# Other hand-written orders for all five engines, and A's transfers ahead of the small vectors

## The chip, the core and the metric

One Trainium2 core runs the whole program. The metric is the device time of one execution in microseconds; lower is better. The program is one launch: a stretch for the first batch, a loop over six middle batches, a stretch for the last.

## The reference

Input x is (8, 1024, 256): eight batches of 1024 rows. All is computed in float32.

```
xn = layernorm(x)                                     # 1e-5
# attention branch, 16 heads of depth 16, no softmax
q = elu(xn @ Wq + bq) + 1 ; k = elu(xn @ Wk + bk) + 1 ; v = xn @ Wv + bv
k = k / sqrt(sum(k*k over a head) + 1e-6)
att = (q k^T) v per head ;  y = xn + (att @ Wo + bo)
a = (y - mean(y)) / sqrt(var(y) + 1e-6) * gamma + beta
# feed-forward branch, three blocks of two quantised linears with low-rank parts
lin_l(h) = h @ dequant(qweights[l], scales[l])^T + biases[l] + (h @ A[l]^T) @ B[l]^T
h = xn
for blk in 0..2:  h = h + lin_{2blk+1}( gelu( layernorm(lin_{2blk}(h)) ) )
out = x + a + h
```

A is `lora_a` (6, 32, 256), B is `lora_b` (6, 256, 32). The codes `qweights` are (6, 256, 256) integers.

## The kernel before

**Tiling.** A batch's 1024 rows lie as eight tiles of 128 rows (`X`, `XN`); a half `h` is four of them, 512 rows. The feed-forward branch works on transposed activations: two 128-channel parts (`m` or `k` = 0, 1) by 512 rows, one PSUM bank each (`FB[h][m]`). Each operand of its products is split into a rounded part and the rest (`xTh`/`xTl`, `hTh`/`hTl`, `gh`/`gl`, `WTh`/`WTl`); `first_high`/`second_high` are eight products of 512 columns with the rounded part, `first_low`/`second_low` four with the rest. Block `j` is `first_*`, squares, variance and its root, normalise, gelu, `second_*`, residual.

**A block's hand-overs.** TensorE `first_high`, `first_low`; ScalarE `square` (L620) for both parts; GpSimd `add_squares` (L417); TensorE `turn_squares` (L1570); VectorE `ffn_var` (L911, L914); GpSimd `ffn_root` (L392); TensorE `spread_rstd` (L1578); ScalarE `rb_copy` (L626); VectorE `ffn_normalise` (L923); ScalarE `gelu` (L630); rounding `g_higher` on VectorE for part 0 (L937) and on ScalarE for part 1 (L635); rest `g_lower` (L262) mostly on GpSimd, some on VectorE; TensorE `second_high` (L1478), `second_low` (L1484); VectorE `ffn_residual` (L932); `h_higher` (VectorE L941, ScalarE L639), `h_lower` (L267). The last block's second product is made row-wise: `rows_state` (L1538), `rows_high` (L1551), `rows_low` (L1561), and `finish` (L1043) adds it into `RES`.

**Attention.** TensorE `project_k(p)` (L1594) for pair p of tiles, ScalarE `k_exp` (L647), VectorE `k_elu` (L948), ScalarE `k_square` (L651), VectorE `k_sum`, `k_rstd` (eleven small instructions), `k_hat` (L982); TensorE `add_g(t)` (L1605) sums K^T xn in bank 4, ScalarE `g_copy` (L656); `make_vk`, `block_diagonal`, `make_m`, `m_copy` build one matrix M per batch; `project_q(h, m)` (L1616), `q_exp` (L663), `q_elu` (L989) make qT; `attend(p)` (L1649) is qT by M. VectorE `att_y(p)` (L1009 to L1020) adds `XNB` and takes the statistics, GpSimd `ln2_root`, VectorE `att_result` (L1029, L1035). GpSimd `base_xn(p)` (L412) makes `XNB` = xn + bo.

**Next batch.** `ln1_statistics`, `ln1_mean_var` (VectorE), `ln1_root` (GpSimd), `ln1_normalise` (ScalarE L611), `xt` (TensorE L1471), `xt_copy` (ScalarE L601, L602) and `xt_lower` (VectorE L1053) of batch i+1 run inside batch i.

**Start.** Weights come once. SyncE issues X, `lora_b`, scales, codes and the projection weights; ScalarE issues seven small vector transfers (`load_vectors`, which waits for one GpSimd constant) and then the four of A (`load_lora`, L580) into `Y`. GpSimd `dequantise` (L430, L435), TensorE `weight_transpose` (L1739 transposes the codes' tile, L1745 adds B A from `lbT` and `Y`), ScalarE `weights_high`, VectorE `weights_low`. `keep_busy` (L1657) is four filler products. `qk_sums` (L1719, L1720) is the column means of Wq and Wk.

**Order.** Nothing is scheduled by the hardware beyond each engine's own list: the functions `head`, `body`, `tail` of every engine name the calls one by one, and semaphores make them wait. Each engine runs its list in order, so a wait holds all behind it. Short-lived results share three rotating PSUM banks and a fourth, the side bank; `HEAD_USES`, `BODY_USES`, `TAIL_USES` list the uses in TensorE's order, `take` (a wait in TensorE for the reader of the bank's last use) and `rotating` derive bank and count from them.

## Time and profile before

| | before |
|---|---|
| median of 3 runs | 616.52 us (616.03 to 617.02) |
| the profiled execution's own time | 616.88 us |
| its span | 615.2 us, 10218 instructions |
| TensorE matmuls | 590.7 us, 96% |
| TensorE weight loads | 498.3 us, 81% |
| VectorE | 526.9 us, 86% |
| ScalarE | 402.8 us, 65% |
| GpSimd | 373.9 us, 61% |
| granted TensorE clock | full in all 40 slices |
| DMA | 29.0 MB, 47 GB/s over the span |

The span is the distance from the first to the last recorded instruction; what lies around it belongs to the execution's time too. A busy share of TensorE near 100% says that it is never without an instruction, not that each is as short as it can be: an instruction that waits inside the pipeline counts as busy. The chain that ended last passes TensorE for 70% of the span, ScalarE for 9%, GpSimd for 7% and VectorE for 6%. In a row of the timeline the columns are the start, the time from the first start to the last end of the merged instructions, the engine, the line, the operation and its tiles, the count, and in brackets the idle time before it with what ended it. In the waits the columns are the total, the number and the longest.

### The profile page before, as it was taken

The numbers are of one execution on the slowest core, as the hardware profiler recorded it, in microseconds if no ns is written. First come the engines' busy times: TensorE is split into PE (matmuls) and PEld (weight loads), VectorE is DVE, ScalarE is ACT, GpSimd is POOL, SyncE is SP. The second block draws the span as 40 slices with busy tenths as digits, with TensorE's granted clock in tenths as the row PEclk, the third lists the DMA queues.
The fourth block names the chain that finished last, engine by engine and source line by source line (L and its number), as shares of the span: only waits on it lengthen the run. The fifth ranks groups of instructions, "written<-read, shape, count | busy, mean of one in ns | idle before, by whom it ended". The sixth has DMA issues, their size and how long they took to land.

```text
span 615.2 us, 10218 instructions
## 1 busy us (share of the span) xinstructions
PE 590.7 (96%) x3285; PEld 498.3 (81%) x3285; DVE 526.9 (86%) x1164; ACT 402.8 (65%) x619; POOL 373.9 (61%) x361
## 2 busy tenths in 40 slices
PE   6999999999999999999999999999999999999986
PEld 5778879778897889868797788978889688987865
DVE  3679899798888989889897988979898898989797
ACT  2776656848667577766768576684876667775552
POOL 5745766557644766457665575556754576746574
PEclk9999999999999999999999999999999999999999
DMA  9103000500032000500004000230004000030001
GB/s 241 62 2 136 1 2 35 170 2 0 1 125 80 0 0 18 180 6 0 0 35 170 0 0 0 87 118 0 0 0 173 32 0 0 34 102 1 0 2 69
DMA packets 11461, 29.00 MB, mean 47 GB/s; under 512 B 2593, under 2 KB 4273, under 8 KB 11441
## 3 DMA queue, kind: packets, MB, share of 16 engines
q1 hardware_dynamic: 10960, 28.35, 13.7%
q10 hardware_dynamic: 480, 0.41, 0.3%
q8 instruction: 10, 0.16, 0.1%
q14 instruction: 11, 0.08, 0.0%
HBM read 20.37 MB, written 8.39 MB: 47 GB/s over the span
## 4 chain that ended last, share of the span: by engine, by line
PE 70%; ACT 9%; POOL 7%; DVE 6%; issue 6%; DMA 1%; ACTq 1%; DVEq 0%; POOLq 0%
PE bank L1478 19%; PE bank L1484 9%; PE bank L1594 7%; PE bank L1605 7%; PE bank L1649 6%; PE bank L1551 4%; PE bank L1616 4%; PE bank L1570 3%; ACT fw L630 3%; POOL gl L262 2%; ACT L630 2%; PE bank L1578 2%; PE bank L1561 2%; PE bank L1538 2%; PE bank L1471 2%
## 5 line engine op out<-in xcount | busy, mean ns | idle before, releaser
L262 POOL TENSOR_TENSOR gl<-fw,gh 128x512 fp32r<-128x512 f32 x80 | 104.2, 1319 | 49.4 <-DVE gh L937 37.5
L417 POOL TENSOR_TENSOR sqs<-fw 128x512 f32<-128x512 f32 x48 | 62.8, 1309 | 73.8 <-ACT fw L620 73.7
L620 ACT ACTIVATE fw<-bank,b1c 128x512 f32<-128x512 f32 x96 | 62.3, 686 | 57.8 <-PE bank L1484 57.8
L630 ACT ACTIVATE fw<-fw,vec 128x512 f32<-128x512 f32 x96 | 74.6, 808 | 14.2 <-DVE fw L923 13.9
L923 DVE SCALAR_TENSOR_TENSOR fw<-bank,b1c,rb 128x512 f32<-128x512 f32 x96 | 67.7, 745 | 16.1 <-ACT rb L626 15.8
L267 POOL TENSOR_TENSOR hTl<-hT,hTh 128x512 fp32r<-128x512 f32 x40 | 54.1, 1368 | 39.8 <-ACT hTh L639 33.0
L392 POOL TENSOR_TENSOR rsf<-vef,neghalf 128x4 f32<-128x4 f32 x48 | 50.6, 1055 | 43.7 <-DVE vef L914 43.0
L1605 PE MATMUL bank<-K,XN 128*128 128x256 f32 x256 | 61.7, 382 | 0.0
L1649 PE MATMUL bank<-M,qT 128*128 128x256 f32 x256 | 59.4, 379 | 0.0
L392 POOL TENSOR_TENSOR rs<-ve,neghalf 128x2 f32<-128x2 f32 (+1 forms) x48 | 41.9, 874 | 22.8 <-DVE ve L1020 17.1
L1605 PEld LDWEIGHTS bank<-K,XN 128*128 128x128 f32 x256 | 46.5, 190 | 7.6 <-DVE K L982 2.0
L1649 PEld LDWEIGHTS bank<-M,qT 128*128 128x128 f32 x256 | 47.2, 190 | 6.1
L626 ACT ACTIVATE rb<-bank 128x512 f32<-128x512 f32 x48 | 28.3, 592 | 35.1 <-PE bank L1578 34.2
L1478 PE MATMUL bank<-gh,WTl 128*128 128x512 f32 x128 | 42.5, 412 | 1.4 <-DVE gh L937 1.4
L1478 PE MATMUL bank<-hTh,WTl 128*128 128x512 f32 x128 | 43.1, 418 | 0.0
L601 ACT ACTIVATE xTh<-bank 128x512 fp32r<-128x512 f32 x32 | 19.2, 599 | 35.8 <-PE bank L1471 35.7
L911 DVE TENSOR_REDUCE bank<-bank 128x4 f32<-128x512 f32 x48 | 33.4, 697 | 10.3 <-PE bank L1570 9.4
L412 POOL TENSOR_TENSOR XNB<-XN,bo_r 128x512 f32<-128x512 f32 x32 | 41.7, 1303 | 0.0
L1478 PE MATMUL bank<-hTh,WTh 128*128 128x512 f32 x128 | 40.3, 396 | 0.0
L1478 PE MATMUL bank<-gh,WTh 128*128 128x512 f32 x128 | 40.2, 395 | 0.0
L1484 PE MATMUL bank<-gl,WTh 128*128 128x512 f32 x128 | 36.9, 410 | 0.0
L1578 PE MATMUL bank<-ident,rsf 128*128 128x128 f32 x192 | 29.0, 274 | 6.8 <-POOL rsf L392 6.8
(157 smaller groups left out, 1593.0 us busy)
## 6 DMA issues: line engine op xcount, KB each, us to landing
X<-in_L_attn_x_dram SPq DMA_DIRECT2D x16, 512.0 KB, 6.7
RES<-in_L_attn_x_dram SPq DMA_DIRECT2D x16, 512.0 KB, 4.3
out_dram<-RES SPq DMA_DIRECT2D x14, 512.0 KB, 2.7
XNB<-in_L_ffn_qweights_dram SPq DMA_DIRECT2D x2, 512.0 KB, 6.6
out_dram<-RES SPq DMA_DIRECT2D x4, 256.0 KB, 2.1
RES<-in_L_ffn_qweights_dram SPq DMA_DIRECT2D x1, 512.0 KB, 8.8
Y<-in_L_ffn_lora_a_dram ACTq DMA_DIRECT2D x4, 96.0 KB, 6.6
Wp<-in_L_attn_Wq_dram SPq DMA_DIRECT2D x1, 256.0 KB, 7.6
```

Of the source, the lines that this page charges most:

```text
L262: engine.tensor_tensor(gl[:, h, m, :], fw[:, h, m, :], gh[:, h, m, :].bitcast(F32), ALU.subtract).then_inc(g_low[h][m], 1)
L267: engine.tensor_tensor(hTl[m][:, half(h)], hT[m][:, half(h)], hTh[m][:, half(h)].bitcast(F32), ALU.subtract).then_inc(h_low[h][m], 1)
L392: return pool.tensor_tensor(dst, var, neghalf[:, 0:n], ALU.pow)
L417: pool.tensor_tensor(sqs[:, h, :], fw[:, h, 0, :], fw[:, h, 1, :], ALU.add).then_inc(sqs_ready[h], 1)
L620: act.activation(fw[:, h, m, :], FB[h][m][:], ACT.Square, bias=b1c[:, m, j:j + 1]).then_inc(sq_ready[h], 1)
L630: act.activation(fw[:, h, m, :], fw[:, h, m, :], ACT.Gelu, bias=lnb[:, m, j:j + 1], scale=lng[:, m, j:j + 1]).then_inc(g_ready[h], 1)
L923: dve.scalar_tensor_tensor(fw[:, h, m, :], FB[h][m][:], b1c[:, m, j:j + 1], rb[:, h, :], ALU.add, ALU.mult).then_inc(yn_ready[h], 1)
L1478: pe.matmul(FB[h][m][:], w[:, l, k, m * P:(m + 1) * P], high, start=(k == 0 and n == 0), stop=False)
L1484: ins = pe.matmul(FB[h][m][:], WTh[:, l, k, m * P:(m + 1) * P], low, start=False, stop=(k == NC - 1))
L1594: ins = pe.matmul(RB[r][:, t * D:(t + 1) * D], x_[k][:, (2 * p + t) * P:(2 * p + t + 1) * P], w[:, k, D:2 * D], start=(n == 0), stop=(n == ...
L1605: ins = pe.matmul(AB[:, c * D:(c + 1) * D], XN[:, t, c * P:(c + 1) * P], K[:, t, :], start=(t == 0 and c == 0), stop=(t == NT - 1), skip_g ...
L1649: ins = pe.matmul(RB[r][:, t * D:(t + 1) * D], qT[c][:, (2 * p + t) * P:(2 * p + t + 1) * P], M[:, c, :], start=(c == 0), stop=(c == NC - 1))
```

## The change

Every engine's three lists get another order; the calls in each list are the same ones, so no instruction and no transfer is added or removed. The three lists of bank uses follow TensorE's new order. In the first batch ScalarE issues `load_lora` ahead of `load_vectors`. SyncE's first-batch list has Wv, Wk and codes 1 ahead of Wq, and bo and gamma later. The middle batch:

```diff
 BODY_USES = [
-    ("k", 0), ("k", 1), ("var", 0, 0), ("rs", 0, 0), ("k", 2), ("k", 3),
+    ("k", 1), ("k", 0), ("var", 0, 0), ("rs", 0, 0), ("k", 2), ("k", 3),
...
@@ sync, head
                 load_small()
                 load_codes(0)
-                load_row(bo_r, bo.unsqueeze(0))
+                load_projection(2, Wv, w_v)
+                load_projection(1, Wk, w_k)
+                load_codes(1)
                 load_projection(0, Wq, w_q)
                 load_out()
-                load_projection(1, Wk, w_k)
-                load_codes(1)
+                load_x(0, 1)
+                load_row(bo_r, bo.unsqueeze(0))
+                load_codes(2)
                 load_row(gamma_r, gamma.unsqueeze(0))
-                load_x(0, 1)
-                load_projection(2, Wv, w_v)
-                load_codes(2)
@@ gpsimd, body
                 ffn_root(i, 0, 0)
+                base_xn(i, 0, BODY)
+                base_xn(i, 1, BODY)
                 add_squares(i, 1, 0)
-                base_xn(i, 0, BODY)
+                base_xn(i, 2, BODY)
                 ffn_root(i, 1, 0)
...
@@ scalar, head
+                load_lora()
                 load_vectors()
-                load_lora()
@@ scalar, body
                 gelu(i, 0, 1, 0)
-                g_copy(i)
                 gelu(i, 0, 1, 1)
                 g_higher(i, 0, 1, 1)
                 rb_copy(i, 1, 1, BODY)
+                g_copy(i)
                 gelu(i, 1, 1, 0)
                 gelu(i, 1, 1, 1)
                 g_higher(i, 1, 1, 1)
+                ln1_normalise(i + 1, 0, BODY)
                 h_higher(i, 0, 1, 0)
                 q_exp(i, 1, 1, BODY)
-                ln1_normalise(i + 1, 0, BODY)
                 m_copy(i, BODY)
@@ vector, body (as it stands after the change)
                 ffn_residual(i, 0, 1, 0, BODY)
                 ln1_mean_var(i + 1, 1)
                 ffn_residual(i, 0, 1, 1, BODY)
                 h_lower(dve, i, 0, 1, 0)
                 h_higher(i, 0, 1, 1)
                 ffn_residual(i, 1, 1, 0, BODY)
                 ffn_residual(i, 1, 1, 1, BODY)
                 h_higher(i, 1, 1, 1)
                 q_elu(i, 1, 1, BODY)
@@ tensor, head
-                keep_busy()
                 lb_transpose()
                 keep_busy()
                 keep_busy()
+                vec_transpose()
                 keep_busy()
-                vec_transpose()
+                keep_busy()
                 weight_transpose(0)
...
+                project_k(0, 3, HEAD)
                 weight_transpose(4)
-                project_k(0, 3, HEAD)
+                second_high(0, 0, 0, HEAD)
+                project_q(0, 1, 0, HEAD)
+                second_low(0, 0, 0)
+                weight_transpose(5)
                 project_q(0, 0, 1, HEAD)
-                weight_transpose(5)
@@ tensor, body
                 add_g(i, 0, BODY)
+                add_g(i, 1, BODY)
                 first_high(i, 0, 1, BODY)
...
-                add_g(i, 1, BODY)
                 turn_squares(i, 0, 1, BODY)
...
+                add_g(i, 5, BODY)
                 turn_squares(i, 1, 1, BODY)
                 spread_rstd(i, 0, 1, BODY)
-                add_g(i, 5, BODY)
                 add_g(i, 6, BODY)
+                project_q(i, 1, 1, BODY)
                 add_g(i, 7, BODY)
                 spread_rstd(i, 1, 1, BODY)
-                project_q(i, 1, 1, BODY)
```

In the last batch TensorE's list moves one q projection between `spread_rstd(i, 1, 0)` and `second_high(i, 0, 0)`; GpSimd's has base_xn(0) to (2) early, base_xn(3) ahead of the second block's g_lower, and `ffn_root(i, 0, 2)` ahead of `add_squares(i, 1, 2)`. In the first batch TensorE's `spread_rstd(0, 0, 0)` moves ahead of `project_k(0, 2)`, and VectorE's `ffn_normalise(0, 0, 2, *)` ahead of `xt_lower(1, 0, 1)`, its `g_higher(0, 0, 2, 0)` ahead of `att_y(0, 2)`.

## Rows read from the trace of the kernel before

**Rows 1.** Busy time of each engine by stretch; then granted clock, DMA share, GB/s

```profile
229.00:301.40 72.40, 71.12 (x397) 60.04 (x396) 63.81 (x142) 49.66 (x77) 44.44 (x41) 1.00 0.13 43
...
591.20:615.20 24.00, 16.75 (x109) 14.12 (x107) 20.14 (x48) 8.04 (x11) 12.72 (x12) 1.00 0.11 44
```

**Rows 2.** Waits of TensorE: total us, times, longest us

```profile
PE bank L1578 <- POOL rsf L392: 6.8, 9, 1.0
```

**Rows 3.** Timeline of the start, the two issuing queues and TensorE

```profile
3.69 1.83 ACTq L580 DMA_DIRECT2D Y<-in_L_ffn_lora_a_dram  x4
...
5.37 1.66 SPq L282 DMA_DIRECT2D Wp<-in_L_attn_Wk_dram  x1
...
6.66 3.62 PE L1657 MATMUL bank<-mean_w,ident 128*128 128x128 f32 x24
...
10.21 0.29 PE L1676 MATMUL bank<-ident,vec_rows 13*128 13x13 f32 x2
...
13.11 1.13 PE L1745 MATMUL bank<-lbT,Y 128*128 128x256 f32 x4 [1.62 <-DMA Y<-in_L_ffn_lora_a_dram]
...
14.95 1.88 PE L1719 MATMUL bank<-Wp,mean_w 128*128 128x512 f32 x4
```

**Rows 4.** DMA issues: KB each, us from issue to landing

```profile
Y<-in_L_ffn_lora_a_dram ACTq DMA_DIRECT2D x4, 96.0 KB, 6.6
...
Wp<-in_L_attn_Wk_dram SPq DMA_DIRECT2D x1, 256.0 KB, 8.2
```

**Rows 5.** Busy time by stretch at the start, columns as in rows 1

```profile
10.00:14.00 4.00, 2.02 (x13) 1.51 (x12) 2.17 (x7) 1.04 (x3) 2.36 (x3) 1.00 1.10 301
```

**Rows 6.** Timeline of TensorE in the first batch and one middle batch

```profile
38.06 0.70 PE L1616 MATMUL bank<-xTh,Wqkl 128*128 128x512 f32 x2 [0.54 <-issue]
...
44.66 0.66 PE L1739 MATMUL bank<-ident,RES 128*128 128x128 f32 x4 [0.84 <-DVE K L948]
...
90.51 0.66 PE L1538 MATMUL bank<-ident,hT 128*128 128x128 f32 x4 [0.75 <-DVE fw L923]
...
94.29 0.38 PE L1551 MATMUL bank<-WTl,gh 128*128 128x256 f32 x1 [0.52 <-DVE gh L937]
...
228.24 0.66 PE L1570 MATMUL bank<-ident,sqs 128*128 128x128 f32 x4 [0.31 <-POOL sqs L417]
...
262.22 0.62 PE L1578 MATMUL bank<-ident,rsf 128*128 128x128 f32 x4 [0.78 <-POOL rsf L392]
263.02 0.70 PE L1478 MATMUL bank<-gh,WTl 128*128 128x512 f32 x2 [0.18 <-DVE gh L937]
...
295.24 0.63 PE L1478 MATMUL bank<-hTh,WTl 128*128 128x512 f32 x2
295.70 0.63 PE L1478 MATMUL bank<-hTh,WTh 128*128 128x512 f32 x2
...
300.68 0.66 PE L1570 MATMUL bank<-ident,sqs 128*128 128x128 f32 x4 [0.31 <-POOL sqs L417]
```

**Rows 7.** Timeline of ScalarE, then VectorE, in the same middle batch

```profile
291.64 0.62 ACT L639 ACTIVATE hTh<-hT 128x512 fp32r<-128x512 f32 x1
...
294.16 2.07 ACT L611 ACTIVATE XN<-X,sh,rs 128x256 f32<-128x256 f32 x4
...
270.55 0.68 DVE L262 TENSOR_TENSOR gl<-fw,gh 128x512 fp32r<-128x512 f32 x1
...
286.88 1.82 DVE L262 TENSOR_TENSOR gl<-fw,gh 128x512 fp32r<-128x512 f32 x1
```

**Rows 8.** Timeline of the last batch: TensorE, GpSimd, VectorE

```profile
552.70 0.71 PE L1478 MATMUL bank<-gh,WTl 128*128 128x512 f32 x2 [0.34 <-DVE gh L937]
...
599.71 0.62 PE L1578 MATMUL bank<-ident,rsf 128*128 128x128 f32 x4 [0.98 <-POOL rsf L392]
...
597.31 1.28 POOL L412 TENSOR_TENSOR XNB<-XN,bo_r 128x512 f32<-128x512 f32 x1
...
611.31 1.27 DVE L1043 TENSOR_TENSOR RES<-bank,RES 128x512 f32<-128x512 f32 x2
```

More of the change, by code:

```diff
@@ L499, in body, with tail @@
                 ffn_root(i, 0, 0)
+                base_xn(i, 0, BODY)
+                base_xn(i, 1, BODY)
                 add_squares(i, 1, 0)
-                base_xn(i, 0, BODY)
+                base_xn(i, 2, BODY)
+                ffn_root(i, 1, 0)
+                g_lower(pool, i, 0, 0, 0)
+                g_lower(pool, i, 0, 0, 1)
+                g_lower(pool, i, 1, 0, 0)
+                h_lower(pool, i, 0, 0, 0)
+                h_lower(pool, i, 0, 0, 1)
+                h_lower(pool, i, 1, 0, 0)
+                h_lower(pool, i, 1, 0, 1)
+                add_squares(i, 0, 1)
+                add_squares(i, 1, 1)
+                ffn_root(i, 0, 1)
+                base_xn(i, 3, BODY)
+                ffn_root(i, 1, 1)
+                g_lower(pool, i, 0, 1, 1)
+                ln1_root(i + 1, 0)
+                g_lower(pool, i, 1, 1, 0)
+                g_lower(pool, i, 1, 1, 1)
+                h_lower(pool, i, 0, 1, 1)
+                add_squares(i, 0, 2)
+                ln2_root(i, 0)
+                ffn_root(i, 0, 2)
+                ln1_root(i + 1, 1)
+                add_squares(i, 1, 2)
+                ffn_root(i, 1, 2)
+                g_lower(pool, i, 0, 2, 1)
+                g_lower(pool, i, 0, 2, 0)
+                ln2_root(i, 1)
+                g_lower(pool, i, 1, 2, 1)
+                g_lower(pool, i, 1, 2, 0)
+                ln2_root(i, 2)
+                ln2_root(i, 3)
+            def tail(i):
+                add_squares(i, 0, 0)
+                base_xn(i, 0, TAIL)
+                ffn_root(i, 0, 0)
+                base_xn(i, 1, TAIL)
+                base_xn(i, 2, TAIL)
+                add_squares(i, 1, 0)
                 ffn_root(i, 1, 0)
@@ L1397, in tail @@
                 ffn_residual(i, 1, 1, 1, TAIL)
+                q_elu(i, 1, 1, TAIL)
                 att_y(i, 0, TAIL)
@@ L1819, in head @@
                 turn_squares(0, 0, 2, HEAD)
+                xt(1, 0, 0, HEAD)
+                first_high(0, 1, 2, HEAD)
+                spread_rstd(0, 0, 2, HEAD)
+                first_low(0, 1, 2)
                 xt(1, 0, 1, HEAD)
-                first_high(0, 1, 2, HEAD)
-                first_low(0, 1, 2)
-                spread_rstd(0, 0, 2, HEAD)
                 attend(0, 2, HEAD)
```

339 lines of the change are left out of this document (148 added, 191 removed), and 18 rows, old and new, of tables (BODY_USES, HEAD_USES, TAIL_USES).

## The prediction, made before the changed kernel ran

> **What bounds the kernel now.** I read the stretches first. In a middle batch TensorE is busy 71.12 of 72.40 us, VectorE 63.81, ScalarE 49.66, GpSimd 44.44, with the DMA engines at a share of 0.13 and the granted clock at 1.00 (the upper level, 2.4 GHz); in the last 24 us TensorE falls to 16.75 while VectorE is busy 20.14 [rows 1]. So three regions have different limits: the start (transfers), the stream up to the last batch (TensorE), the last 20 us (VectorE). TensorE's waits come next: the largest is for the reciprocal roots of GpSimd, 6.8 us in nine waits [rows 2]. An engine order can only win what TensorE waits, so I then looked for each wait in the timeline and asked which order stands ahead of it.
>
> At the start the four transfers of A are issued at 3.69 us, behind seven small ones. TensorE has turned the first weight's codes and then idles 1.62 us for A, until 13.11; the column sums over Wq and Wk start at 14.95 [rows 3]. A takes 6.6 us from issue to landing, Wk 8.2 [rows 4]: issued at 5.37 [rows 3], Wk lands at about 13.6, hardly before it is needed. From 10 to 14 us the DMA engines move 301 GB/s at a busy share of 1.10 [rows 5]: they have no time left. The whole start is limited by transfer.
>
> **The change, part by part.** No instruction is added or removed; each engine's list holds the same calls in another order, and the same bytes move. The sum is one of waits.
>
> *Start.* A now stands first in ScalarE's list and needs no constant, so its first issue moves from 3.69 to about 1. With the same 6.6 us to landing, and some for the sharing, the last of it is there at 8 to 10.5, so the 1.62 us at 13.11 goes [rows 3, 4]. What is late next? First, Wq: SyncE now issues it behind Wv, Wk and the second pair of codes. Ahead of its landing stand 512 KB of codes more and 128 KB of bo less than stood ahead of Wk before, 384 KB or 393 thousand bytes; at the 301 GB/s of [rows 5] that is 1.3 us, so Wq lands at 13.6 + 1.3 = 14.9 against column sums that began at 14.95. Second, the vector rows (biases, gamma, beta) now follow A on ScalarE's queue, and TensorE turns them before two of its four filler groups; before, they were turned at 10.21 with no wait [rows 3]. If they land at 11 instead of by 10.2, the two fillers (three groups took 3.62 us, so 1.2 each [rows 3]) end at 13.7 and the first weight's work ends 1 us later than before. Bounds of the whole start: a gain of 1.6, if neither is late, and a loss of 1.0. I take a gain of 0.3, since the Wq estimate lies nearest to no change and TensorE can do the bias means and transposes no sooner than those sums.
>
> The Trainium skill, "DMA: Bandwidth & Descriptors", section "Issuing engines are not separate DMA queues", says that DMAs issued by different engines run on the same 16 DMA engines and interleave, and that a second issuer saves only issue time. By that rule A's early landing is paid by X, lora_b and the first codes. The share of 1.10 agrees [rows 5]. Taken alone, it would make the start's term zero where the wait of 1.62 us taken alone would make it 1.6.
>
> *Middle of the first batch.* TensorE waits before its projection of q (0.54) and before transposing weight 5 (0.84) [rows 6]. The second wait stands because that transpose takes the side bank right behind project_k(3), and so waits for k_elu(3), itself behind a table load on ScalarE. In the new order second_high, another q projection and second_low of half 0 stand between them: at 1.87, 1.4 and 0.93 us (eight, six and four 512-column products; two of them take 0.46 us from start to start in [rows 6]) that is 4.2 us of cover. spread_rstd(0,0,0) moves ahead of project_k(2), which takes away the pair of root transposes ahead of the first wait. Both waits, 1.38 us, should go; something is late instead where second_high now asks early for gelu's result. I take 1.2 (bounds 0 and 1.4).
>
> *End of the first batch.* TensorE waits 0.75 for VectorE's normalise of half 0 (rows_state) and 0.52 for its rounding of g [rows 6]. VectorE now does the normalise ahead of one xt_lower and the rounding ahead of att_y(2), which is the longest item there. Of 1.27 us I take 0.8 (bounds 0 and 1.3).
>
> *Six middle batches.* These decide, because everything counts six times. The marked idle of TensorE is 0.31 + 0.78 + 0.18 = 1.27 us in a batch [rows 6], the 1.28 that [rows 1] leaves; six times that, 7.6 us, is the most that new orders can win here beyond small slips inside busy time. The 0.78 and 0.18 hang on project_k(3), k_exp(3), a table load, gelu and the rounding, with ScalarE's and VectorE's lists unchanged at that place; they stay. The 0.31 (turn_squares behind first_low, square, add_squares) is covered by attend(0) and one transpose in both orders; it stays. Gains: add_g(1) now covers the rounding of h, and one xt_lower stands earlier; unmarked both, bounded by one such wait, 0.31, of which I take 0.1. Losses: ScalarE does ln1_normalise (2.07) before h_higher(0,1,0), which started at 291.64 before; VectorE's h_lower and h_higher stand behind it in order. With 0.68 for each of the two VectorE steps (an upper bound for the rounding) 291.64 + 2.07 + 0.62 + 0.68 + 0.68 = 295.69, while TensorE's first_high starts at 295.24 and wants the second half of h four products later, 0.93 us, at 296.17 [rows 6, 7]. The slack is about 0.5 us; the price is nothing while ScalarE reaches ln1_normalise no later than 0.5 us past the time at which it reached h_higher. q_elu(1,1) also moves behind more work and the bank of attend(0) waits for it; its slack I put near zero, but the 0.31 stands right behind it and absorbs as much. I take a loss of 0.07, net gain 0.03 a batch, 0.2 in all (bounds: a loss of 0.8 and a gain of 0.6 each).
>
> *base_xn moved.* GpSimd did base_xn(1) beside VectorE's g_lower, which took 1.82 us there and 0.68 where GpSimd was not on a large tile [rows 7]. In the new order base_xn(0) and (1) stand where GpSimd waited for ScalarE's squares of half 1. Price nothing, as long as both fit; if not, up to 0.1 a batch.
>
> *Last batch.* Another q projection (about 1.4 us) now stands between spread_rstd(1,0) and second_high(0,0), which waited 0.34 [rows 8]; the wait for the root ahead of it stays. At the end GpSimd did base_xn(3) (1.28) before ffn_root(1,2), and TensorE waited 0.98 for that root [rows 8]. But VectorE runs there almost without a gap, so TensorE's wait isn't worth its length: ffn_root(0,2) ahead of add_squares(1,2) and the earlier normalise remove perhaps 0.5 of VectorE's own idle time, up to its last add at 611.31 [rows 8]. 0.3 + 0.5 = 0.8 (bounds 0 and 1.5).
>
> *Sum.* 0.3 + 1.2 + 0.8 + 0.2 + 0.8 = 3.3 us. The profiled execution took 616.88 us, its span 615.2 and 1.7 around it: 613.6. The median of the runs shown is 0.36 below it, so 613.2; I say 613.3.
>
> **Rivals.** (1) *The middle batches slow down*: the one mechanism is ScalarE's h_higher(0,1,0) behind ln1_normalise. The new order also puts spread_rstd(0,1) behind another add_g and so starts ScalarE's whole gelu run later; if ScalarE arrives 1.3 us late, 0.8 past the slack comes back six times, 4.8 us: 618.1. It decides at 0.5. For it: VectorE is busy 63.8 of 72.4, so a late start isn't made up quickly [rows 1]. Against: g_copy moves behind that run and gives its own length back. (2) *The start is starved and VectorE eats the first batch's gain*: start at a loss of 1, middle and end of the first batch together 1.0, rest as forecast 1.0: 615.5. For it: the share of 1.10 in [rows 5]; against: TensorE has other work, the transposes of codes and x, that doesn't wait for Wq. (3) *The middle batches get faster too*: the late root (0.78) is partly a matter of GpSimd. If VectorE, freed of 1.14 us beside base_xn [rows 7], brings its results forward and 0.6 of the 1.27 goes, six times 0.6 is 3.6: 609.7. Against: VectorE's next step there waits for ScalarE's copy anyway. The Trainium skill, "GPSIMD Engine Reference", section "1. Specifications", says that GpSimd's SBUF interfaces are shared with VectorE and that VectorE's instructions with two SBUF inputs or in a two-port mode contend; by that rule this third way is the one, and the 1.82 against 0.68 agrees with the contention, not with its reaching TensorE. (4) *A isn't what comes last* and its move does nothing: the start gives 0, the rest 3.0, 613.6; not told apart from the forecast by time.
>
> **How the numbers follow.** Forecast, with (4): 0.53, own range 611.5 to 615.2. (1) 0.17, 615.5 to 620. (2) 0.17, 614.5 to 616.5. (3) 0.13, 608.5 to 611.5. What a measurement of this kernel tells from no change is about 0.2%, 1.2 us. Below 615.3: 0.50 + 0.13 + 0.08 + 0.02 = 0.73. Above 617.7: 0.10 of (1) and 0.02 for sums of bad ends, 0.12. Between: 0.15. The range 610.3 to 617.3 leaves out half of (3) and most of the upper half of (1).
>
> **What would show it.** TensorE's wait on A gone, with its column sums still near 14.9; if they start by 13.8, the start gave 1. No wait before weight 5. The distance of two turn_squares(0,2) is 72.44 us now (300.68 less 228.24 [rows 6]); it should be 72.3 to 72.6, and 73 or more is rival (1), 71.9 or less rival (3). In the last batch no base_xn behind 590. The forecast is wrong if a wait on Wq, on the vector rows, or on ScalarE's rounding of h appears among TensorE's waits.

## The result, and the profile after the change

The changed kernel takes 617.83 us (median of 20 runs, 616.92 to 618.47); the kernel before, timed beside it, 616.85 (20 runs, 616.03 to 617.74). The ratio is 1.0014, with a 95% interval of 1.0007 to 1.0020: some 0.9 us slower, where 3.3 us less were forecast. The median lies above the predicted range, which ended at 617.3. By its absolute time it also lies just above 617.7, a case that had a chance of 0.12; measured against the kernel before it stays within 0.2%, the case that had 0.15. Every timed run of every kernel is used but one: of the last kernel of the experiments, c5, one run of ten took 2073 us and is left out of its ratio.

The profiled execution took 618.35 us, 1.47 more than the one of before, with a span of 616.5. The medians differ by 0.98 only, so about half a microsecond of the 1.47 is chance; the experiments show that the start is what varies. The busy time by stretch first, for the same middle batch as in [rows 1] and for the end, then the stretches of the first batch in which TensorE had waited. Columns are PE, weight load, VectorE, ScalarE, GpSimd, granted clock, DMA share, GB/s.

```profile
229.00:301.40 72.40, 71.14 (x398) 60.01 (x397) 63.13 (x142) 49.83 (x76) 44.73 (x41) 1.00 0.13 43
591.20:616.50 25.30, 16.62 (x110) 14.28 (x109) 20.82 (x47) 8.04 (x11) 11.60 (x11) 0.94 0.11 42
...
34.00:60.00 26.00, 26.00 (x144) 21.59 (x143) 23.66 (x51) 21.26 (x31) 15.49 (x14) 1.00 0.17 57
80.00:102.00 22.00, 21.72 (x143) 19.08 (x142) 19.93 (x50) 14.12 (x24) 13.45 (x15) 1.00 0.06 25
```

The middle batch is what it was: 71.14 us of TensorE in 72.40, before 71.12 [rows 1]. The granted clock of 0.94 in the row of the end has no part in the result: the clock is 1.00 up to 612 us, and 0.85 and then 0.50 behind it, where TensorE has no work left. In the first batch TensorE is busy without a gap from 34 to 60, so the waits of 0.54 and 0.84 [rows 6] are gone, and the later pair of 0.75 and 0.52 leaves 0.28 of idle time. What got worse is at the two ends. The start, from the timeline of TensorE, VectorE and the two issuing queues:

```profile
8.04 0.87 PE L1665 MATMUL bank<-ident,lb 128*128 128x128 f32 x3 [8.04 <-DMA lb<-in_L_ffn_lora_b_dram]
8.70 3.62 PE L1657 MATMUL bank<-mean_w,ident 128*128 128x128 f32 x16
12.25 0.39 PE L1676 MATMUL bank<-ident,vec_rows 13*128 13x13 f32 x2
12.57 2.09 PE L1657 MATMUL bank<-mean_w,ident 128*128 128x128 f32 x16
14.49 0.60 PE L1739 MATMUL bank<-ident,XNB 128*128 128x128 f32 x4
14.93 1.03 PE L1745 MATMUL bank<-lbT,Y 128*128 128x256 f32 x4
...
16.67 1.88 PE L1719 MATMUL bank<-Wp,mean_w 128*128 128x512 f32 x4
...
6.04 1.41 DVE L896 BATCH_NORM_STATS2 st<-X 128x6 f32<-128x256 f32 x4 [6.04 <-DMA X<-in_L_attn_x_dram]
```

A isn't waited for any more, but TensorE now does nothing until lora_b lands at 8.04. Before, it began at 3.46 with a filler (L1657, products whose result nobody reads) and turned lora_b at 5.99 [rows 3]. x comes 1.0 us later as well (VectorE's statistics at 6.04; 5.05 before). All four fillers (x8 in the rows is one) now stand between lora_b and the first weight, and the column sums over Wq and Wk (L1719) start at 16.67, before at 14.95 [rows 3].

The last batch, again from the timeline: TensorE's two waits in its first half, the turning and spreading behind the last block's first layer, and the end of GpSimd and VectorE.

```profile
551.83 0.62 PE L1578 MATMUL bank<-ident,rsf 128*128 128x128 f32 x4 [1.13 <-POOL rsf L392]
559.21 0.70 PE L1478 MATMUL bank<-gh,WTl 128*128 128x512 f32 x2 [1.16 <-DVE gh L937]
...
595.42 0.62 PE L1578 MATMUL bank<-ident,rsf 128*128 128x128 f32 x4 [0.62 <-POOL rsf L392]
596.66 0.63 PE L1570 MATMUL bank<-ident,sqs 128*128 128x128 f32 x4 [0.62 <-POOL sqs L417]
599.61 0.62 PE L1578 MATMUL bank<-ident,rsf 128*128 128x128 f32 x4 [0.59 <-POOL rsf L392]
...
605.15 2.52 POOL L262 TENSOR_TENSOR gl<-fw,gh 128x512 fp32r<-128x512 f32 x2
...
606.45 1.25 DVE L1020 TENSOR_SCALAR ve<-mv 128x2 f32<-128x2 f32 x1
607.61 1.27 DVE L1043 TENSOR_TENSOR RES<-bank,RES 128x512 f32<-128x512 f32 x2
...
613.35 0.69 DVE L1043 TENSOR_TENSOR RES<-bank,RES 128x512 f32<-128x512 f32 x1
```

The rounding of g that TensorE waited 0.34 for [rows 8] is now waited for 1.16. In the second half its three waits for GpSimd's sums and roots are 0.62, 0.62 and 0.59, together 1.83; before they were 0.39, 0.35 and the 0.98 of [rows 8], together 1.72: the long one went, and the sum didn't. The last add ends at 613.35 + 0.69 = 614.04; before at 611.31 + 1.27 = 612.58 [rows 8].

To split the difference up I cut each execution at three places that exist in all of them: the first product of the first layer (L1478 on the rounded xT) in the first, the second and the last batch. In the two profiled executions these start at 20.73, 102.29 and 536.73 before, and at 22.55, 102.07 and 536.36 after:

| stretch | before | after | difference | forecast |
|---|---|---|---|---|
| start, to the first product | 20.73 | 22.55 | +1.82 | −0.3 |
| first batch, to the product in the second | 81.56 | 79.52 | −2.04 | −2.0 |
| six middle batches | 434.44 | 434.29 | −0.15 | −0.2 |
| last batch, to the end of the last add | 75.85 | 77.68 | +1.83 | −0.8 |

Their sum is +1.46, the 1.47 between the two executions. Two of the four terms came as forecast, two were wrong in sign.

### The profile page after: what moved, and what is told of

It reads as the page before. It is cut to its first block, busy times and chain, and to the rows that moved or that the text cites. A ratio compares the mean times of both kernels' runs of the same rounds, so it can differ in the third digit from the quotient of the medians.

```text
span 616.5 us, 10218 instructions
## 1 busy us (share of the span) xinstructions
PE 589.8 (96%) x3285; PEld 497.9 (81%) x3285; DVE 522.0 (85%) x1164; ACT 403.9 (66%) x619; POOL 374.9 (61%) x361
## 4 chain that ended last, share of the span: by engine, by line
PE 71%; issue 9%; POOL 8%; DVE 6%; ACT 4%; DMA 1%; POOLq 0%; SPq 0%; DVEq 0%; ACTq 0%
PE bank L1478 19%; PE bank L1484 9%; PE bank L1605 8%; PE bank L1594 7%; PE bank L1649 6%; PE bank L1616 4%; PE bank L1551 4%; POOL gl L262 3%; PE bank L1570 3%; PE bank L1561 2%; PE bank L1578 2%; PE bank L1538 2%; PE bank L1471 2%; ACT L630 1%; POOL hTl L267 1%
## 5 line engine op out<-in xcount | busy, mean ns | idle before, releaser
L392 POOL TENSOR_TENSOR rs<-ve,neghalf 128x2 f32<-128x2 f32 (+1 forms) x48 | 40.3, 840 | 31.6 <-DVE ve L1020 20.7
L1478 PE MATMUL bank<-gh,WTl 128*128 128x512 f32 x128 | 43.5, 421 | 2.2 <-DVE gh L937 2.2
L412 POOL TENSOR_TENSOR XNB<-XN,bo_r 128x512 f32<-128x512 f32 x32 | 44.1, 1388 | 0.0
L1478 PE MATMUL bank<-hTh,WTl 128*128 128x512 f32 x128 | 42.5, 413 | 0.0
L1478 PE MATMUL bank<-hTh,WTh 128*128 128x512 f32 x128 | 40.2, 395 | 0.0
L1478 PE MATMUL bank<-gh,WTh 128*128 128x512 f32 x128 | 40.2, 395 | 0.0
```

The costliest lines, as they stand in the source:

```text
L392: return pool.tensor_tensor(dst, var, neghalf[:, 0:n], ALU.pow)
L412: pool.tensor_tensor(XNB[:, 2 * p:2 * p + 2, :], XN[:, 2 * p:2 * p + 2, :], bo_r[:].unsqueeze(1).broadcast_to([P, 2, D]), ALU.add).then_in ...
L1478: pe.matmul(FB[h][m][:], w[:, l, k, m * P:(m + 1) * P], high, start=(k == 0 and n == 0), stop=False)
```

## The experiments

Every kernel was timed in five rounds beside the kernel before. The last batch is where the most experiments went: there the orders of all five engines changed, ScalarE's and VectorE's too, more than the moves that the description of the change lists. The stretches are worked out from each profiled execution's own timeline like those above. "Column sums" is the start of L1719.

| kernel | lora_b turned | column sums | first batch | loop | last batch | ratio to before (95%) |
|---|---|---|---|---|---|---|
| before | 5.99 | 14.95 | 81.56 | 434.44 | 75.85 | |
| changed | 8.04 | 16.67 | 79.52 | 434.29 | 77.68 | 1.0014 (1.0007 to 1.0020) |
| e1 only A first | 7.42 | 15.66 | 81.55 | 434.51 | 75.78 | 1.0019 (1.0008 to 1.0031) |
| e2 A second again | 6.12 | 14.86 | 79.56 | 434.52 | 77.75 | 0.9993 (0.9983 to 1.0003) |
| e3 old last batch | 7.25 | 16.51 | 79.57 | 434.44 | 76.41 | 0.9995 (0.9985 to 1.0006) |
| e4 only the last batch new | 6.04 | 15.51 | 81.61 | 434.45 | 77.72 | 1.0037 (1.0021 to 1.0054) |
| c1 = e2 and e3 | 6.16 | 15.26 | 79.57 | 434.27 | 76.39 | 0.9987 (0.9978 to 0.9996) |
| e5 one filler first | 7.31 | 16.14 | 79.55 | 434.36 | 77.71 | 1.0015 (1.0004 to 1.0026) |
| c2 = c1, Wv late | 5.98 | 15.07 | 79.53 | 434.41 | 76.40 | 0.9966 (0.9954 to 0.9978) |
| c3 = c2, two fillers fewer | 6.06 | 15.54 | 79.55 | 434.38 | 76.39 | 0.9968 (0.9954 to 0.9981) |
| c4 = c2, one filler first | 6.11 | 13.66 | 79.56 | 434.38 | 76.41 | 0.9974 (0.9963 to 0.9985) |
| t1 VectorE's end old | 7.22 | 15.68 | 79.56 | 434.36 | 79.36 | 1.0045 (1.0031 to 1.0059) |
| t2 GpSimd's end old | 7.17 | 15.41 | 79.57 | 434.29 | 77.37 | 1.0013 (1.0004 to 1.0023) |
| t4 rounding first | 7.25 | 16.06 | 79.57 | 434.37 | 78.37 | 1.0015 (1.0007 to 1.0024) |
| t5 = t4 and both ends old | 7.28 | 15.72 | 79.54 | 434.40 | 78.19 | 1.0020 (1.0010 to 1.0030) |
| m1 = c2, first half new | 6.07 | 14.98 | 79.56 | 434.42 | 76.56 | 0.9977 (0.9968 to 0.9986) |
| m2 = c2, second half new | 6.06 | 14.22 | 79.54 | 434.30 | 80.40 | 1.0046 (1.0031 to 1.0061) |
| t6 new, but turning first | 5.97 | 14.44 | 79.57 | 434.40 | 77.66 | 0.9994 (0.9985 to 1.0004) |
| t7 = m1, spreading first | 6.17 | 14.71 | 79.55 | 434.39 | 76.81 | 0.9992 (0.9982 to 1.0001) |
| c5 = c4, A in the middle | 6.42 | 15.13 | 79.61 | 434.29 | 76.36 | 0.9976 (0.9967 to 0.9986) |

The middle columns repeat to 0.1 us and better; the start of one kernel differs by more from one execution to the next (the start of e4 is that of before, and its column sums come 0.56 later). A stretch can be read from one profile, then, a start only where several agree. With A first lora_b was turned between 7.17 and 8.04 in the eight profiled executions, with A second between 5.97 and 6.17 in all eleven (c5 has A between the two groups of small transfers).

**e1 and e2: A's place.**

```
             def head():
-                load_vectors()
                 load_lora()
+                load_vectors()
```

> The kernel before with one edit: ScalarE issues the four transfers of A ahead of its seven small ones. Theory 1 (what A's early place costs is paid by lora_b and x): TensorE's transpose of lora_b starts near 8.0 us instead of 5.99, VectorE's first statistics near 6.0 instead of 5.05; the wait of 1.62 us on A is gone, and the column sums start between 14.5 and 15.5, so the time stays within 0.6 us of before. Rival (SyncE's new order is what delays lora_b and x in the changed kernel): lora_b stays near 6.0 here, the column sums start near 13.5, and the time falls by 1.0 to 1.6 us.

> The changed kernel with ScalarE's seven small transfers ahead of A again, all else new. Theory 1: lora_b and x land as in the kernel before (6.0 and 5.05), TensorE begins 2 us sooner and ends its four fillers near 12.5 instead of 14.5, then waits for A until about 13; column sums near 15 instead of 16.67, and the time is 1.0 to 1.7 us below the changed kernel, so 0.0 to 0.7 below before. Rival (SyncE's order): lora_b stays near 8.0 and the time is the changed kernel's, within 0.4 us.

TensorE's start in e1:

```profile
3.46 2.08 PE L1657 MATMUL bank<-mean_w,ident 128*128 128x128 f32 x8 [3.46 <-POOL head_mask L386]
7.42 0.87 PE L1665 MATMUL bank<-ident,lb 128*128 128x128 f32 x3 [1.89 <-DMA lb<-in_L_ffn_lora_b_dram]
8.09 4.15 PE L1657 MATMUL bank<-mean_w,ident 128*128 128x128 f32 x24
...
13.26 0.63 PE L1739 MATMUL bank<-ident,XNB 128*128 128x128 f32 x4 [0.80 <-POOL XNB L435]
```

Alone, the title's half of the change loses: 1.0019, a little more than the 0.6 us that I had expected. The wait for A (1.62) is gone, one of 1.89 for lora_b and one of 0.80 for the dequantised codes stand in its place; SyncE's order is untouched here, so it isn't the cause. The chain that ends last has changed its link: GpSimd, done with its other work, sat idle for 1.38 us until the first codes had landed and began with them at 11.29, before at 8.88. e2 gives the counterpart, 0.9993 for all of the change but A's place. From 1.0014 to 0.9993 is 1.3 us.

e2 also shows that A needn't have been moved. TensorE makes the product with A at 12.48, with no more than 0.2 us of waiting in a weight load, though A is issued at 3.69 as before:

```profile
11.95 0.60 PE L1739 MATMUL bank<-ident,XNB 128*128 128x128 f32 x4
12.48 1.13 PE L1745 MATMUL bank<-lbT,Y 128*128 128x256 f32 x4
```

With SyncE's old list A came later: TensorE waited for it until 13.11 in the kernel before and until 13.67 (1.95 us) in e4. In c4 below, which has the TensorE start of the kernel before but a new list of SyncE's, the product with A starts at 11.69. In none of the nine profiled kernels with A second and a new list of SyncE's does the product wait for A, in both with the old list it does. So the new order of SyncE's transfers took the wait of 1.62 away without A's early place.

**e3, e4, c1: the last batch.** e3 takes the last batch's orders of all five engines from the kernel before, e4 makes only these new, c1 undoes both losing parts.

> The changed kernel with the orders of the last batch, on all five engines, taken from the kernel before. Theory: the last batch's new orders cost 1.7 us (from first_high of the last batch to the last add it takes 77.6 us in the changed kernel and 75.8 before), so the time is 1.2 to 1.9 us below the changed kernel: 615.9 to 616.6. Rival (the last batch is slower because of how it is entered, from the new loop orders): less than 0.5 us below the changed kernel.

> The kernel before with only the last batch's orders new, on all five engines. Theory (the last batch's order by itself is worse): 1.2 to 1.9 us above before. Rival (worse only together with the new loop's orders): within 0.5 us of before, or faster, as the prediction had it with 0.8.

> The changed kernel with both losing parts undone: ScalarE's seven small transfers ahead of A again, and the last batch's orders of the kernel before. What is left is the new order of the first batch and of the loop. If the parts add, the gain of undoing each (1.1 us for A's place, 0.9 to 1.4 for the last batch) gives 617.8 - 1.1 - 1.2 = 615.5 us, faster than before by 1.3 us. If they do not add (the wait on VectorE's end returns whatever TensorE wins), it stays within 0.4 us of before.

The new last batch takes 77.7 whichever loop is ahead of it, so its loss is its own. The old one takes 76.4 behind the new loop and 75.8 behind its own; 0.3 of the 0.6 is a wait of TensorE, near its beginning, for VectorE's last add of the batch before (L1043), which isn't there in the kernel before. c1 is faster than before (0.9987, 0.8 us). The parts don't quite add in the medians: undone singly, they gave 1.3 and 1.2 us; together, 1.7. The intervals of these ratios are 0.8 us wide and more, so this is no proof that the parts interact.

**t1, t2, t4, t5: single suspects in the last batch.** t1 puts VectorE's last sixteen steps back, t2 GpSimd's last four, t4 exchanges two lines of VectorE's list (L1366 and the next), t5 does all three.

```
-                k_rstd(i)
                 g_higher(i, 1, 0, 0)
+                k_rstd(i)
```

> The changed kernel with VectorE's last sixteen steps of the last batch in the order of the kernel before: the third attention tile's sum ahead of both normalise steps of half 1, and each finished pair one place later. Theory 1 (VectorE's own order costs the last batch 1.3 to 1.8 us, because the sums of the last two attention tiles stand behind normalise steps that wait for TensorE's late second root): 1.0 to 1.6 us below the changed kernel. Rival 2 (GpSimd's two large tiles back to back, ahead of the last root, are the cause): less than 0.4 us below it.

> The changed kernel with GpSimd's last four steps of the last batch in the order of the kernel before: one rounding remainder, both last roots, one remainder. Theory 1 (VectorE's order is the cause): within 0.4 us of the changed kernel. Rival 2: the small step of VectorE that took 1.25 us behind two large GpSimd tiles takes 0.17 again, and the time falls by 0.8 to 1.3 us.

> The changed kernel with one exchange in VectorE's list of the last batch: its rounding of g for half 1 ahead of the step for k's norms, a chain of small operations, as in the kernel before. Theory (this exchange is what put 1.15 us of TensorE's waiting into the last batch, where before it was 0.34, and the batch's end moves with it): TensorE's wait for that rounding falls to about 0.3, the last batch, from its first product to the last add, takes 76.6 to 77.0 instead of 77.7, and the time falls by 0.7 to 1.1 us below the changed kernel. Rival (TensorE's wait goes, but VectorE, which limits the end, does the same work in the same time): wait gone, last batch within 0.3 us of 77.7.

> The changed kernel with that exchange and with the ends of VectorE's list (sixteen steps) and of GpSimd's (four) together in the order of the kernel before. Taking VectorE's end alone made the last batch 1.7 us longer, since GpSimd's last root then stood behind a rounding remainder that VectorE and ScalarE made late. Theory (the two ends belong together, and with the exchange they are what the new last batch lost): the last batch takes 75.9 to 76.5 us, the time is 1.2 to 1.8 below the changed kernel. Rival (TensorE's new order there, a root's spreading ahead of the turning of the other half's squares, is what counts): above 76.9.

Each of my theories of a single culprit fell. t1 made the batch 1.7 us longer: GpSimd does its last root behind two remainders in the new list, and with VectorE's old order the g that these need comes late.

```profile
607.81 2.78 POOL L262 TENSOR_TENSOR gl<-fw,gh 128x512 fp32r<-128x512 f32 x2 [3.20 <-ACT gh L635]
610.56 0.87 POOL L392 TENSOR_TENSOR rs<-ve,neghalf 128x2 f32<-128x2 f32 x1
```

In t4 TensorE's wait for the rounding did go, but two others came (0.68 for ScalarE's rounding of h, 0.20 for its remainder on GpSimd), and the batch grew by 0.7. t2 is the one whose last batch became shorter: with the large tiles parted by the roots, the small VectorE step takes 0.17 instead of 1.25, and the batch 77.37. Its ratio of 1.0013 doesn't show the 0.3 us.

```profile
603.55 1.29 POOL L262 TENSOR_TENSOR gl<-fw,gh 128x512 fp32r<-128x512 f32 x1 [0.71 <-DVE gh L937]
604.80 1.45 POOL L392 TENSOR_TENSOR rs<-ve,neghalf 128x2 f32<-128x2 f32 x2
...
605.30 0.17 DVE L1020 TENSOR_SCALAR ve<-mv 128x2 f32<-128x2 f32 x1
...
606.22 1.26 POOL L262 TENSOR_TENSOR gl<-fw,gh 128x512 fp32r<-128x512 f32 x1
...
606.59 1.57 DVE L1029 SCALAR_TENSOR_TENSOR Y<-Y,mv,gamma_r 128x256 f32<-128x256 f32 x2
```

Of the 1.08 us that the small step gave back, 0.70 went elsewhere: the two steps L1029 beside GpSimd's other remainder take 1.57 here and 0.87 in the changed kernel.

**m1, m2, t6, t7: by halves.** m1 and m2 cut all lists at the making of M. t7 is m1 with the exchange below (GpSimd's and VectorE's steps that belong to it go along); t6 undoes only that exchange in the new last batch.

```
                 attend(i, 1, TAIL)
-                turn_squares(i, 1, 2, TAIL)
                 spread_rstd(i, 0, 2, TAIL)
+                turn_squares(i, 1, 2, TAIL)
```

> The kernel with Wv late, in the last batch all engines' new orders up to the making of M and the old ones from the first attention tile on. With the old orders throughout, the last batch takes 76.4 us after the new loop; with the new ones 77.7. Theory 1 (the second half holds the loss: a root spread ahead of the other half's turning, VectorE's normalise steps ahead of its attention sums): 76.4 to 76.8 here. Rival 2 (the first half holds it: TensorE waited 1.13 and 1.15 us there, against 0.77 and 0.34): 77.3 to 77.8.

> The same cut, the other way: old orders up to the making of M, new ones from the first attention tile on. Theory 1 (second half holds the loss): the last batch takes 77.1 to 77.7 us. Rival 2 (first half): 76.3 to 76.7.

> The kernel with Wv late and A behind the small transfers, with the new last batch but for one thing undone on three engines: TensorE turns half 1's last squares before it spreads half 0's roots, GpSimd adds half 1's squares before half 0's root, VectorE takes half 1's variance before half 0's normalise. Theory S (spreading first is the loss: half 1's squares were turned 60.3 us into the last batch instead of 58.8): the last batch takes 76.5 to 76.8 us. Theory F (the finishing order of VectorE and GpSimd is the loss): 77.3 to 77.7.

> The kernel with the new orders up to the making of M and the old ones behind it, in which the last batch took 76.56 us, with only that exchange made on the three engines: spreading ahead of turning. Theory S: 77.2 to 77.7 us. Theory F: 76.4 to 76.8.

m1 is the clearest: it has both long waits of the new first half, and its last batch takes 76.56 against 76.40 with the old half.

```profile
550.33 0.62 PE L1578 MATMUL bank<-ident,rsf 128*128 128x128 f32 x4 [1.13 <-POOL rsf L392]
557.71 0.70 PE L1478 MATMUL bank<-gh,WTl 128*128 128x512 f32 x2 [1.14 <-DVE gh L937]
...
610.13 1.28 DVE L1043 TENSOR_TENSOR RES<-bank,RES 128x512 f32<-128x512 f32 x2
```

So 2.27 us of waiting, 1.17 more than c2 has there (0.77 and 0.33), cost 0.16. The loss is in the second half, and there little of it in spreading ahead of turning: t7 pays 0.25 for that, t6 wins nothing by undoing it (77.66). What is left, 1.1 us by t6 against m1 or 0.9 by the new batch (77.7) against t7, belongs to the finishing order of VectorE and GpSimd with TensorE's rows; one exchange in ScalarE's list (its rounding of g behind `rb_copy`) and the place of q_elu(1,1) went along in every such pair and weren't tested alone.

The rows of VectorE say where the time is. From 56.0 us into the last batch to the end of its last add it is idle 2.02 of 21.68 us in the changed kernel and 1.23 of 20.56 in m1. Of the 0.79 more, 0.37 is its wait for the second attention tile (0.66, in m1 0.29). Another 0.51 is this wait, and 0.11 a gap before the last add, where m1 has one of 0.19 for a root instead:

```profile
609.60 0.87 DVE L1035 SCALAR_TENSOR_TENSOR RES<-Y,rs,RES 128x256 f32<-128x256 f32 x2
610.98 0.69 DVE L1043 TENSOR_TENSOR RES<-bank,RES 128x512 f32<-128x512 f32 x1 [0.51 <-DVE RES L1035]
```

Here an add stands directly behind the `att_result` whose `RES` it needs; in the old order other steps stand between. All eight profiled kernels with VectorE's new end have this 0.51, and none with the old end has it. The other 0.33 is busy time: the 1.08 of the small step is the largest item in it, and m1 has one of 0.44 against it, its own last pair of L1029 (1.31 for 0.87). No run takes out one of these alone, so they say where the time is spent and not what each would give back. m2 isn't a fair counterpart: at the cut VectorE's q_elu(1,1) moves ahead of h's rounding while ScalarE still has the old order, TensorE waits 2.14 for that rounding, and the batch takes 80.40. It shows again that the lists don't mix.

**e5, c2, c3, c4: fillers and transfers in the start.**

> The changed kernel, A still first, with one more of TensorE's fillers than the four it had and one of these ahead of the transpose of lora_b, as in the kernel before (one, then three). Theory 1 (the fillers behind lora_b are on the path: four of them and the transposes took from 8.04 to 14.49, the first eight columns groups at half pace because TensorE had been idle until then): one filler from 3.46 on changes little of the pace; five in all, three behind lora_b and one more behind the vectors' transpose would end near 14.0 to 14.5, so the time is within 0.6 us of the changed kernel. Rival (the idle time before lora_b is what costs): column sums by 15.5 and 1 us less.

(This expectation miscounts: the kernel has four fillers in all, one ahead of lora_b and three behind.)

> The kernel with the new orders of the first batch and the loop, ScalarE's seven small transfers ahead of A and the last batch of before (615.8 against 616.55 in its own comparison), and SyncE now loads Wq and Wk first, then the second codes and x, and Wv and Wo behind them. Theory (the column sums wait for the fillers, not for a transfer): the first weight is turned at the same time, near 12 to 13, and the time is within 0.4 us of that kernel. Rival (Wq and A land late behind Wv): 0.5 to 1.0 us less.

> The kernel just described without the two groups of filler products that stand behind the turning of the vectors (they compute nothing that is used). Theory (the fillers are on the path, the first weight's codes being ready near 11.05): the first weight is turned near 11.1, the column sums start 1.0 to 1.8 us sooner and the time falls by 0.8 to 1.5 us below that kernel: 614.3 to 615.0 where before has 616.6. Rival (without the fillers TensorE's products stay at the slower pace of the first microseconds, and what is won is lost): within 0.4 us of it, with the products of the first weight taking twice as long.

> The kernel with Wv late (A behind the seven small transfers, old last batch), with one of TensorE's four fillers moved ahead of the transpose of lora_b, so that TensorE begins at 3.46 instead of 6.0, and the rest in the order of the kernel before. Without two fillers the first weight was turned at 11.1 but its products took twice as long and nothing was won. Theory (work from 3.46 on brings TensorE to its full pace before the first weight): the first weight is turned near 11.1 at full pace, its four products take 1.0 and not 2.1 us, the column sums start near 14.0 instead of 15.1, and the time falls by 0.6 to 1.1 us: 613.9 to 614.4 where before has 617. Rival (A, landing near 12 to 13, is the limit again): a wait on A, and within 0.4 us.

TensorE in c3 (two fillers taken out), then in c4 (four fillers, one of them ahead of lora_b):

```profile
11.09 1.09 PE L1739 MATMUL bank<-ident,XNB 128*128 128x128 f32 x4 [0.43 <-POOL XNB L435]
12.15 2.07 PE L1745 MATMUL bank<-lbT,Y 128*128 128x256 f32 x4
...
15.54 1.88 PE L1719 MATMUL bank<-Wp,mean_w 128*128 128x512 f32 x4
```

```profile
3.45 2.08 PE L1657 MATMUL bank<-mean_w,ident 128*128 128x128 f32 x8 [3.45 <-POOL head_mask L386]
...
11.14 0.63 PE L1739 MATMUL bank<-ident,XNB 128*128 128x128 f32 x4 [0.34 <-POOL XNB L435]
11.69 1.13 PE L1745 MATMUL bank<-lbT,Y 128*128 128x256 f32 x4
...
13.66 1.88 PE L1719 MATMUL bank<-Wp,mean_w 128*128 128x512 f32 x4
```

Without the fillers the first weight is turned at 11.09 instead of 12.89, but its four products take 2.07 and not 1.03: nothing is won. With one filler from 3.45 on it is turned as early, at full pace, and the column sums start at 13.66, the earliest of all. c4's profiled execution is the shortest (span 612.5), yet its timed runs don't follow: median 614.96 (614.23 to 616.89), c2 614.97. With A first the same edit (e5) has the column sums at 16.14, within the 15.41 to 16.67 of the six other kernels with that start, and the ratio of the changed kernel. c2 against c1 went the other way: the profiles are alike, the ratio falls from 0.9987 to 0.9966. Four more kernels share c2's start, m1, t6, t7 and m2; less what their last batches take beyond 76.40, their ratios are 0.9977 - 0.0003 = 0.9974, 0.9994 - 0.0020 = 0.9974, 0.9992 - 0.0007 = 0.9985 and 1.0046 - 0.0065 = 0.9981, and the column sums of the five start between 14.22 and 15.07. So c2's own ratio is the low end of a scatter, and Wv's late place is worth between nothing and 0.1%.

One more kernel issued the four rows of vectors, then A, then the three biases. (Its edit moves three lines of `load_vectors` behind `load_lora`.)

> The kernel just described, with ScalarE's list starting with the four small transfers of the vector rows, then the four of A, then the three of the attention biases: A is issued from near 2.0 us instead of 3.7. Theory (whatever A gains is taken from lora_b and x as soon as they share the queue's first microseconds): lora_b lands 0.5 to 1.2 us later than 6.0 and the time is within 0.5 us of the kernel just described. Rival (A before 3.7 costs nothing as long as it is behind lora_b): lora_b stays near 6.0, any wait on A goes, and up to 0.8 us is won.

A went out at 2.30 and lora_b was turned at 6.42; the column sums started at 15.13 and the ratio is 0.9976 (0.9967 to 0.9986), as c4's. Nearer to the theory, with a smaller delay of lora_b than it said (0.3 against c4); no gain.

## Why the prediction was wrong, step by step

*Start, −0.3 forecast, +1.8 in this profile.* Outside its own bounds. The term that failed is this gain of 0.3, with its bounds of a gain of 1.6 and a loss of 1.0. The prediction priced A, Wq and the vector rows, but never asked what TensorE waits for first. That is lora_b, whose row stood in the profile ([rows 3]: TensorE's first work at 3.46, and what follows lora_b at 6.66), and the new list has no filler ahead of it any more. A's 384 KB, issued from 0.79 on, push lora_b from 6.0 to between 7.2 and 8.0. In the changed kernel the fillers, the vectors and the first codes follow it without a wait, so there it is lora_b that sets the start; in e1 it is the first codes, another of those that A pushed back. A filler put back ahead of lora_b (e5) doesn't help as long as A is first. The two delays that the prediction feared didn't come: Wq, issued at 6.33, was there 7.6 us later, at 13.9, ahead of its 14.9, and the vector rows were turned at 12.25 without a wait. The prediction quoted the rule of the Trainium skill, "DMA: Bandwidth & Descriptors", section "Issuing engines are not separate DMA queues", that such transfers interleave on the same engines, and wrote that x, lora_b and the first codes would pay. It then took zero as the worst that this could do. The payers' own rows had to be priced: each has a first user, and lora_b's was TensorE itself. The trace agrees with the rule: with nothing changed but A's place (e1), lora_b, x and the codes all came later. By chance part of the 1.8 is this execution's: in the other seven with A first lora_b came 0.6 to 0.9 earlier, and the medians differ by 1.0 where the profiled executions differ by 1.5. A's place by itself costs 1.2 to 1.3 us in the ratios of e1 and e2.

*Middle and end of the first batch, −2.0 forecast, −2.04 measured*, and the same 79.5 in all kernels with the new order, 81.6 in those without. The waits named went, and no new one came. Here TensorE is the bound, so a covered wait is a gain. Between its two terms, 1.2 and 0.8, no experiment tells.

*Middle batches, −0.2 forecast, −0.15 measured.* The distance of two turnings of squares is 300.33 - 227.91 = 72.42 us (72.44 before), inside the 72.3 to 72.6 of the forecast. Rival (1) had its mechanism right and its price too high: ScalarE does ln1_normalise first, at 291.63, h_higher at 293.60 instead of 291.64 [rows 7], and VectorE's next step on h waits for it.

```profile
227.91 0.66 PE L1570 MATMUL bank<-ident,sqs 128*128 128x128 f32 x4 [0.17 <-POOL sqs L417]
300.33 0.66 PE L1570 MATMUL bank<-ident,sqs 128*128 128x128 f32 x4 [0.19 <-POOL sqs L417]
...
291.63 2.07 ACT L611 ACTIVATE XN<-X,sh,rs 128x256 f32<-128x256 f32 x4
293.60 0.62 ACT L639 ACTIVATE hTh<-hT 128x512 fp32r<-128x512 f32 x1
...
294.25 0.69 DVE L267 TENSOR_TENSOR hTl<-hT,hTh 128x512 fp32r<-128x512 f32 x1 [0.95 <-ACT hTh L639]
294.86 0.42 DVE L941 TENSOR_SCALAR hTh<-hT 128x512 fp32r<-128x512 f32 x1
...
294.89 0.63 PE L1478 MATMUL bank<-hTh,WTl 128*128 128x512 f32 x2
```

The rounding ends at 295.28; TensorE's use of the second half of h, two rows further, starts at 295.82: a slack of 0.54, as the 0.5 that the prediction worked out. ScalarE arrived on time and nothing was lost. Rival (3), VectorE freed of GpSimd, came on VectorE only: it is busy 63.13 us in the batch, 0.68 less than before, and TensorE's wait for the root is 0.77, before 0.78.

*Last batch, −0.8 forecast, +1.8 measured.* Two errors. In the first half I took 0.3 for a wait that would go; instead it grew from 0.34 to 1.16, since VectorE's list has `k_rstd`, eleven small operations of 0.2 to 0.6 us, ahead of the rounding that TensorE wants. I had read TensorE's list there and not VectorE's. That error cost nothing (m1, 0.16), for the reason that I had given only for the second half: VectorE sets the end of this batch, and TensorE's waits are absorbed. The second error is the one that counts. I priced a reordering of VectorE's, GpSimd's and TensorE's last steps by the idle time that it could remove (bounds 0 and 1.5) and gave it no way to add any. From 56 us into the batch on, VectorE is idle 0.79 us more in the changed kernel than in m1, 0.51 of it in one add behind the step it depends on, and one of its small steps stands 1.08 longer beside GpSimd's large tiles.

*The rivals.* Rival (4), A not being what comes last, is out for the kernel before, which waited 1.62 for it. It is half right for the new lists, in which A second isn't waited for either (e2). Rival (2), a start that is starved and eats the gain, is the nearest: right in kind, with a loss of 1.0 where 1.8 came in the profile and some 1.2 in the medians. That the last batch could lose was no rival at all, and it is half of the miss.

What stays open: which exchange in the last batch's finishing order would give back the remaining 0.6 to 0.8 us beyond the 0.3 of t2, since the rows of VectorE name the places and no run undoes one alone; and why c4's shorter start isn't seen in its median, for which the pace of TensorE's first microseconds, told below, is the nearest candidate. The best of these kernels take 614.8 to 615.0 us, by their ratios 0.3% below the kernel before: the new first batch and loop, the old last batch, A behind the small transfers, and Wv and Wo behind what the start needs.

## What to carry to other kernels

A transfer that is moved forward on a saturated start is paid by those already there: list the first user of each of them, above all of the one that the busiest engine waits for first, before the move is priced. Two changes that aim at one wait are to be priced apart: here SyncE's new list had already removed what A's early place was to win. Read a wait's worth from the region: where TensorE is the bound it comes back in full (2.0 of 2.0), where VectorE is, 1.17 us more of TensorE's waiting cost 0.16. Orders of several engines that were made together are one object: putting one engine's list back made the batch up to 1.7 us longer, and a bound of "zero at worst" isn't to be had for a reordering on the engine that sets the end.

## What the runs showed of the hardware

TensorE's pace in the first microseconds isn't constant. In the changed kernel, idle until 8.04, the sixteen filler products of the first row take 3.62 us, the sixteen of the next 2.09, and the profile gives the granted clock as 1.00, the upper level, over both stretches (columns as above):

```profile
8.60:12.20 3.60, 3.60 (x18) 3.43 (x16) 0.42 (x1) 2.07 (x4) 2.78 (x5) 1.00 1.08 357
12.50:14.50 2.00, 2.00 (x19) 1.97 (x19) 1.82 (x6) 0.00 (x0) 1.92 (x3) 1.00 1.07 384
```

In c3 the first weight's four products take 2.07, in c4 1.13. The slow pace is seen in durations alone. In c3's profile, taking out two of the four fillers gained nothing, since the products behind them were slow in their place. The pace also varies from one execution to the next. From the first of the four fillers behind lora_b to the turning of the first codes, with no wait marked between, it is 5.17 us in e2 and 6.41 in e3, and between these in the eleven other profiled kernels with that list. With one filler ahead of lora_b the three behind it take 3.62 (before), 3.80 (c4), 4.15 (e1), 4.21 (e4), 4.96 (c5) and 5.08 us (e5). The 1.2 us of the first spread is about as much as the column sums of equal starts differ by, so c4's early 13.66 may in part be a lucky execution. The Trainium skill, "TensorE: Matmul & The Clock Gate", section "What's actually happening", has an idle array at 1.2 GHz and says that the number of slow products varies from run to run. A factor near two (2.07 against 1.03) agrees with the first and the spread above with the second; that this is why c4's median shows no gain, no run here shows.

A VectorE step of 128x2 elements took 1.25 us while GpSimd ran two 128x512 remainders back to back (2.52 us), and 0.17 in t2, where small roots stood between them. The Trainium skill, "GPSIMD Engine Reference", section "1. Specifications", says that the two engines share their SBUF interfaces and names VectorE's two-port and two-input instructions as those that contend; this step has one input, and whether it runs in the two-port mode no run here tells. Steps with two SBUF inputs are stretched beside GpSimd's tiles too, as the page has it: the pair L1029 takes 0.87 alone, 1.57 in t2 and 1.31 in m1.
